# First attention: statistics begun a batch ahead, projections by part, and a top-k prologue laid into its last steps; second attention: values by chunk

## The chip, the cores and the metric

The kernel runs on one core of one Trainium2 chip. The core has five engines with a queue of instructions each: PE (TensorE, matrix products), DVE (VectorE), ACT (ScalarE), POOL (GpSimd) and SP (SyncE, which only issues transfers); they wait for one another through semaphores. The metric is the time of one launch on the device in microseconds; lower is better. All data is float32 unless a row says f16.

## The reference

A two-layer language-model tower over 4 sequences of 512 tokens with 128 features:

```python
h = tok(x, ids, numeric)                 # table rows gathered, added, + a small MLP
h = h + attn0(layernorm(h))              # 8 heads of 16; logits from qk and a distance (below)
h = h + topk_ffn(layernorm(h))           # 8 heads, 64 + 64 keys, top 8 of 64: 64 of 4096 rows per token
h = h + attn1(layernorm(h))              # 8 heads of 64, softmax in f32
h = h + moe(layernorm(h))                # 16 experts, each takes its top 64 tokens
# attn0:
omega = (q2[:, None] + k2[None, :] - 2*qk) / (exp(-nf_q) + 1)
A = softmax(qk / sqrt(16) - omega)       # nf_q: |Q - mean| summed, over Q's standard deviation
```

Here q2 and k2 are sums of squares over the 16 features of a head.

## The kernel before

A batch below is one sequence (B = 4), a tile is 128 tokens (TPB = 4 tiles a batch, 16 in all). The stages follow one another: a prologue (gathers, embedding, layer norm and projection of batch 0), the first attention, the top-k layer, the second attention, the experts. Each engine's program is one list written by hand; nothing reorders it. What an engine does beside the main loop is tied to a step number g or to u, the step within a batch, so an item that is not ready makes everything behind it on that engine wait.

**First attention.** It has 64 row steps, 16 a batch (STEPS0). In row step g PE makes the logits of 128 queries with 512 keys for two heads (L1529), DVE takes the two row maxima (L1038; PE's step g waits for the first maximum of step g-1). Twelve steps later (SHIFT) PE makes the same logits as columns with the maxima put in (L1533), and ACT takes their exps (L691, two a step). Values times weights (pv0, L1551) go into every second step. So row steps are 0 to 63, column steps 12 to 75, and steps to END0 = 84 finish the outputs. One PSUM bank, bank 7, is shared by all side work, one item a step, named in the table BANK7_0: `xnT` (transposed layer norm), `qkv` (projection), `k`, `q`, `q2` (transposes of the augmented operands), `back`, `fwd`, `out` (output), `tile` (a tile for the top-k layer). PE's next item waits until another engine has emptied the one before (first_bank7_free).

For each batch from 1 on the path is: gathered rows are added to h (POOL add_tokens, L492 and L494, for batches 2 and 3; DVE embed_tokens for 0 and 1); layer norm (DVE ln_stats L937, POOL's power L471, POOL normalise0 L478 or DVE ln_scale L949); PE transposes and projects it, one tile of q, k and v together at a time; ACT copies it out (copy_raw); POOL adds the biases with 12 instructions (L516) and computes mean, deviation, variance and the sums of squares (query_keys, L391 to L397), and a power for the standard deviation (sigma0, L484); DVE and ACT make the factors of nf_q; only then can PE transpose the augmented keys (L1485) and queries (L1491) of the batch.

**Top-k layer.** A tile needs its key scores (L1626, L1627), eight maxima and their indices (DVE), the inner products with 32 groups of down rows (L1689; ACT's relu frees their two banks), one-hot masks (one_v L1229, w_v L1235, one_u L1241) and the products that use them (`spread`, L1709). Tile t+1's front part goes beside tile t; the front parts of tiles 0 and 1 stand ahead of the loop.

**Second attention.** It has 64 steps: PE's logits (L1751), DVE's maximum (L1327), ACT's exps (L859), POOL's division (L621), PE's transposes (L1762), which ACT (L868) and DVE (L1341) evacuate. After every fourth step stand the 8 products of values of two heads (pv1, L1776), then ACT copies them (outT1, L875). Projections of the next batch and layer norms (L949) lie at fixed u.

## Time and profile before

| | |
|---|---|
| runs of the kernel | 1163.49 us median of 3 (1157.9 to 1167.11) |
| profiled execution | 1167.85 us, of which its span 1166.0 |
| mean granted TensorE clock | 0.92 |
| busy share of PE / DVE / ACT / POOL | 84% / 70% / 43% / 36% |
| first attention, row steps | 48.73 to 239.03 us |
| its rest and the first masks of the top-k layer | 239.03 to 308.70 us |
| second attention | 729.34 to 1014.80 us |

All starts are microseconds from the start of the span. Busy time says how long an engine had an instruction under way; PE's instructions overlap, so 84% does not say that it runs at its peak. "Granted clock" is the share of TensorE's full clock that the chip allowed it in that stretch: 1.00 is the higher of two levels (2.4 GHz), 0.50 the lower (1.2 GHz).

### The profile page before, as it was taken

Reading aid. Unit: us, or ns where it says so; the run is one execution under the profiler, and the core shown is the slowest. Engines: PE = TensorE matmul, PEld = TensorE weight load, DVE = VectorE, ACT = ScalarE, POOL = GpSimd, SP = SyncE. Lnnn points to the kernel's source line nnn. Section 1 sums busy time; section 2 is a strip of 40 time slices with the busy share of each in tenths; the row PEclk is TensorE's granted clock in tenths of the full one; section 3 lists DMA queues with packets and bytes.
Section 4 is the critical chain, followed back from the end, with each engine's and each line's share of the span. In section 5 each row is a group of like instructions: output and inputs, shape, how many; then the busy total and the mean of one; then the engine's idle time right before and its main releaser. Section 6 shows DMA issues by size and latency. Waiting matters only on the chain.

```text
span 1166.0 us, 21877 instructions
## 1 busy us (share of the span) xinstructions
PE 976.9 (84%) x8088; PEld 691.4 (59%) x8088; DVE 814.8 (70%) x2576; ACT 500.0 (43%) x1045; POOL 424.0 (36%) x398
## 2 busy tenths in 40 slices
PE   3486788897788889888888877899999988789997
PEld 3344344444577878777788875545455554367775
DVE  5655657655799999999999953565655565352887
ACT  1114445543434334444443332556555654335332
POOL 5468726200343343445333340445444453300000
PEclk9577889997799999999999998889999998879999
DMA  4000300000000000000000011000000000000000
GB/s 106 9 19 17 147 1 1 2 1 1 2 1 1 2 2 1 2 1 2 1 1 2 2 38 73 1 1 1 1 1 1 1 1 1 1 1 1 10 9 18
DMA packets 6720, 14.11 MB, mean 12 GB/s; under 512 B 1885, under 2 KB 4766, under 8 KB 6046
## 3 DMA queue, kind: packets, MB, share of 16 engines
q1 hardware_dynamic: 5598, 10.70, 2.8%
q0 software_dynamic: 1024, 2.10, 0.7%
q8 instruction: 62, 1.02, 0.4%
q14 instruction: 36, 0.29, 0.1%
HBM read 11.74 MB, written 1.05 MB: 11 GB/s over the span
## 4 chain that ended last, share of the span: by engine, by line
PE 49%; DVE 30%; issue 7%; ACT 6%; POOL 4%; POOLq 2%; DVEq 1%; DMA 0%; SPq 0%; ACTq 0%
PE bank L1776 5%; PE quad L1869 5%; PE bank L1864 5%; DVE w_v L1235 5%; PE quad L1751 4%; DVE i L1152 4%; PE bank L1762 3%; PE quad L1709 3%; PE bank L1529 3%; DVE one_u L1241 3%; PE bank L1720 3%; ACT a_e L859 2%; DVE a_negmax L1327 2%; PE bank L1689 2%; PE bank L1551 2%
## 5 line engine op out<-in xcount | busy, mean ns | idle before, releaser
L621 POOL TENSOR_TENSOR a_e<-a_e,a_rrec 128x1024 f32<-128x1024 f32 x64 | 121.2, 1893 | 165.8 <-DVE a_rrec L1334 165.7
L586 POOL TENSOR_TENSOR vals<-relu_in,g_sb 128x512 f32<-128x512 f32 x80 | 125.3, 1609 | 152.4 <-DVE one_u L1241 129.4
L1689 PE MATMUL bank<-xnT,wd 128*128 128x128 f32 x1024 | 136.8, 291 | 37.0 <-ACT relu_in L739 36.3
L1689 PEld LDWEIGHTS bank<-xnT,wd 128*128 128x128 f32 x1024 | 126.8, 201 | 45.0 <-ACT relu_in L739 43.9
L1720 PE MATMUL bank<-wu,vals 128*128 128x128 f32 x1024 | 118.7, 277 | 4.9 <-issue 4.9
L1720 PEld LDWEIGHTS bank<-wu,vals 128*128 128x128 f32 x1024 | 117.3, 194 | 4.9 <-issue 4.9
L859 ACT ACTIVATE a_e<-quad,a_negmax 128x512 f32<-128x512 f32 x128 | 86.9, 684 | 59.7 <-DVE a_negmax L1327 57.1
L1327 DVE TENSOR_REDUCE a_negmax<-quad 128x2 f32<-128x1024 f32 x64 | 77.7, 1215 | 42.3 <-PE quad L1751 41.4
L691 ACT ACTIVATE a_eT<-quad 128x512 f32<-128x512 f32 x128 | 69.6, 596 | 79.2 <-PE quad L1533 79.2
L1529 PE MATMUL bank<-a_kT,a_qT 32*128 32x512 f32 x344 | 88.4, 468 | 17.1 <-DVE a_q_aug L1038 10.9
L739 ACT ACTIVATE relu_in<-bank 128x512 f32<-128x512 f32 x128 | 73.2, 593 | 40.0 <-PE bank L1689 39.6
L1869 PEld LDWEIGHTS quad<-wu,hidT 128*128 128x128 f32 x512 | 67.6, 194 | 31.3 <-issue 27.8
L1533 PE MATMUL quad<-a_q2T,a_kT 32*128 32x512 f32 x512 | 83.8, 447 | 2.7 <-ACT a_eT L691 2.6
L1038 DVE TENSOR_REDUCE a_q_aug<-bank 128x1 f32<-128x512 f32 x86 | 57.1, 685 | 36.4 <-PE quad L1529 19.0
L1751 PE MATMUL quad<-a_kT,a_qT 64*128 64x512 f32 x512 | 79.1, 429 | 2.6 <-ACT a_e L859 1.9
L1762 PE MATMUL bank<-ident,a_e 128*128 128x128 f32 x512 | 72.8, 287 | 7.9 <-DVE a_eT L1341 4.3
L1709 PE MATMUL quad<-w_v,one_u 128*128 128x64 f16 x2048 | 70.9, 194 | 9.9 <-DVE one_u L1241 8.1
L1709 PEld LDWEIGHTS quad<-w_v,one_u 128*128 128x128 f16 x2048 | 65.9, 98 | 20.4 <-DVE one_u L1241 12.5
L1529 PEld LDWEIGHTS bank<-a_kT,a_qT 32*128 32x128 f32 x344 | 50.4, 213 | 44.1 <-DVE a_q_aug L1038 28.6
L1762 PEld LDWEIGHTS bank<-ident,a_e 128*128 128x128 f32 x512 | 57.5, 145 | 32.0 <-issue 22.6
L1241 DVE TENSOR_TENSOR one_u<-iota_u,uv 128x2048 f16<-128x2048 f16 x64 | 73.9, 1213 | 0.0
L1751 PEld LDWEIGHTS quad<-a_kT,a_qT 64*128 64x128 f32 x512 | 44.8, 191 | 47.9 <-issue 35.6
(238 smaller groups left out, 1944.1 us busy)
## 6 DMA issues: line engine op xcount, KB each, us to landing
wd<-in_pk_down SPq DMA_DIRECT2D x1, 2048.0 KB, 7.9
wu<-in_pk_up SPq DMA_DIRECT2D x1, 2048.0 KB, 12.5
wu<-in_moe_w SPq DMA_DIRECT2D x2, 1024.0 KB, 5.8
out<-h SPq DMA_DIRECT2D x4, 256.0 KB, 2.3
wd<-in_num_rows SPq DMA_DIRECT2D x1, 512.0 KB
a_eT<-in_pk_wqT SPq DMA_DIRECT2D x1, 512.0 KB, 7.1
a_eT<-in_pk_keys SPq DMA_DIRECT2D x1, 512.0 KB, 8.6
wu<-in_event_table,idx_e POOLq DMA_INDIRECT x16, 2.6
```

The lines of the kernel that those rows point to most:

```text
L586: nc.gpsimd.tensor_tensor(*weigh_args(t, c, k, g_sb[:, slot, :])).then_inc(vals_pool, 1)
L621: nc.gpsimd.tensor_tensor(e1[:, g % 4], e1[:, g % 4], rrec1[:, g % 4].unsqueeze(2).to_broadcast([P, 2, S]), ALU.mult).then_inc(a1.nr, 1)
L859: nc.scalar.activation(e1[:, g % 4, r, :], quad[:, 2 * (g % 2) + r, :], ACT.Exp, bias=negmax1[:, g % 4, r:r + 1], accum_out=rowsum1[:, g % ...
L1241: V.tensor_tensor(one_u[:, c * n:(c + 1) * n], iota_u[:].unsqueeze(1).to_broadcast([P, n, NU, 2]), token_pairs(uv[:, t % 2, 0, c * GT:(c + ...
L1327: V.tensor_reduce(negmax1[:, g % 4], quad[:, 2 * (g % 2):2 * (g % 2) + 2, :], AX.X, ALU.max, negate=True).then_inc(a1.mx, 1)
L1529: row = mm(bank[S1_BANKS[(2 * g + r) % 3]], qT0[part, qp, gr % 2, j * P:(j + 1) * P], kT0[part, kp, gr % 4, :], start=(n == 0), stop=(n == 3))
L1689: last = mm(bank[g % 2][:, q * P:(q + 1) * P], wd[:, IG * g + q, :], xnT_tile(t), start=True, stop=True)
L1709: made = mm(quad[:, 2 * (c % 2) + i // half_pair, cols], one_u[:, pair // 2, :, pair % 2], w_v[:, pair // 2, k, :, :, pair % 2].rearrange( ...
L1720: last = mm(bank[6][:, 0:D], vals[:, v, :], wu[:, v, :], start=(v == 0), stop=(v == NV - 1))
L1751: last = mm(quad[:, 2 * (g % 2) + r, :], qT1[rows, qp, p, j * P:(j + 1) * P], kT1[rows, kp, p, :], start=(n == 0), stop=(n == len(parts) - 1))
L1762: last = tp(bank[r][:, c * P:(c + 1) * P], e1[:, g % 4, r, c * P:(c + 1) * P], ident[:])
L1869: last = mm(bank[2 + e % 2][:, j * D:(j + 1) * D], hidT[:, e % 2, j * P:(j + 1) * P], w2e[:, e, :], start=True, stop=True)
```

## The change

- Projections of the first attention go by part: first q of all four tiles, then k, then v, with a semaphore for each; POOL adds one bias a part (three instructions of 128x512 a batch for twelve of 128x128). The shared-bank items of a batch move to earlier steps.
- POOL no longer adds gathered rows (add_tokens) nor normalises (normalise0): DVE does both, for batch 1 ahead of the loop, for batches 2 and 3 at steps 6, 12, 19 and 21. The two sums of squares go from POOL to DVE (square_sums, u = 7). POOL's gathers of batch 2 come right after the statistics of batch 1, its gathers of batch 3 after scale_queries(1).
- ACT's copy out of bank 7 stands between the two exps of a step.
- Into batch 3 and the steps after it go the transposes and scores of the top-k tiles 0, 1 and 2; into steps 66 to 73 the inner products of tile 0, one group of four a step. DVE's maxima and indices of tiles 0 and 1 spread over steps 64 to 79.
- Second attention: the values of a pair of heads are multiplied a chunk at a time, two products in each of four steps instead of eight in one; the copy of the sums moves one pair later and the output projection from u = 4 to u = 7.

```diff
-            {2: ("xnT", 1), 3: ("qkv", (1, 0)), 5: ("qkv", (1, 1)), 6: ("qkv", (1, 2)), 7: ("qkv", (1, 3)),
...
+            {0: ("xnT", 1), 1: ("qkv", (1, 0)), 2: ("qkv", (1, 1)), 3: ("qkv", (1, 2)), 9: ("q2", 0), 10: ("k", 2),
+             12: ("k", 3), 13: ("xnT", 2), 14: ("qkv", (2, 0)), 15: ("q", 2)},
...
+            {1: ("q2", 3), 2: ("back", 1), 4: ("fwd", 0), 5: ("q", 5), 6: ("out", 0), 8: ("k", 6), 9: ("q2", 4),
+             10: ("back", 2), 12: ("k", 7), 15: ("q", 6)},
+            {1: ("q2", 5), 2: ("back", 3), 3: ("tile", 0), 4: ("fwd", 1), 5: ("q", 7), 6: ("out", 1), 7: ("score", (0, 0)),
+             8: ("score", (0, 1)), 9: ("q2", 6), 10: ("back", 4), 11: ("tile", 1), 12: ("score", (1, 0)),
+             13: ("score", (1, 1))},
+            {1: ("q2", 7), 2: ("back", 5), 4: ("fwd", 2), 6: ("out", 2), 7: ("tile", 2), 8: ("score", (2, 0)),
+             9: ("score", (2, 1)), 10: ("back", 6), 12: ("uvp", 0), 15: ("back", 7)},
...
+        EARLY_INNER = range(ALL0 + 2, ALL0 + 2 + NG)
...
-        V1_AT = {3: 0, 7: 1, 10: 2, 11: 3}
+        V1_AT = {3: 0, 10: 1, 11: 2, 14: 3}
...
-            if u == 4 and 0 < b < B:
+            if u == 7 and 0 < b < B:
...
-            def add_tokens(b):
-                span = slice(b * S, (b + 1) * S)
-                pool.wait_ge(gath[b], 16 * 2 * TPB)
-                pool.wait_ge(h_early, b + 1)
-                nc.gpsimd.tensor_tensor(ev_rows[:, span], ev_rows[:, span], vv_rows[:, span], ALU.add)
-                pool.drain()
-                nc.gpsimd.tensor_tensor(h[:, span], h[:, span], ev_rows[:, span], ALU.add).then_inc(h_ready, 1)
...
-            def add_qkv_bias(b):
+            def add_qkv_bias(b, part, dst, done):
+                pool.wait_ge(a0.raw, 3 * (b - 1) + part + 1)
+                nc.gpsimd.tensor_tensor(dst, raw0[:, part], qkv_bias(part), ALU.add).then_inc(done, 1)
...
+            def query_keys(b):
                 pool.wait_ge(aug_clear, 1)
+                pool.wait_ge(a0.q_aug, b)
+                add_qkv_bias(b, 0, q4[:], a0.q_biased)
+                pool.drain()
+                sum_by_halves(pool, st0[:, 0], q4, dev)
                 pool.wait_ge(a0.k_ps, GROUPS * b)
...
-                sum_by_halves(pool, st0[:, 0], q4, dev)
+                add_qkv_bias(b, 1, k_aug[:, :, :, 0:DH0], a0.k_biased)
...
-                pool.wait_ge(a0.squares, 2 * b + 1)
-                sum_by_halves(pool, k_aug[:, :, :, K2], k2, k2).then_inc(a0.k_aug, 1)
                 sigma0(b)
-                pool.wait_ge(a0.squares, 2 * b + 2)
-                sum_by_halves(pool, st0[:, 8], q2, q2).then_inc(a0.q2, 1)
+                if b >= 3:
+                    pool.wait_ge(a0.pv, GROUPS * TPB * (b - 2))
+                add_qkv_bias(b, 2, v0[:, b % 3, :, :, 0:DH0], a0.v_biased)
+                if b >= 2:
+                    pool.wait_ge(a0.q2_ps, GROUPS * (b - 1))
+                nc.gpsimd.memset(q_aug[:, b % 2, :, :, TOPMOST], 0.0)
...
             rstd_step(lnB, 1, TPB)
-            normalise0(1)
-            add_bias0(0)
             gather(2)
             query_keys(1)
-            add_tokens(2)
+            rstd_step(lnB, 2, TPB)
             scale_queries(pool, nc.gpsimd, 1)
-            rstd_step(lnB, 2, TPB)
-            normalise0(2)
             gather(3)
-            add_tokens(3)
+            add_bias0(0)
             add_bias0(1)
             rstd_step(lnB, 3, TPB)
             query_keys(2)
             add_bias0(2)
+            add_bias0(3)
             scale_queries(pool, nc.gpsimd, 2)
             query_keys(3)
-            add_bias0(3)
...
-            def exp0(s):
...
+            def exp0(s, r):
                 pair, c = s // TPB, s % TPB
...
+                if r == 0:
+                    act.wait_ge(a0.cols, s + 1)
+                    if pair >= 3:
+                        act.wait_ge(a0.pv, (pair - 3) // 2 * TPB + c + 1)
+                nc.scalar.activation(eT0[:, pair % 3, r, c, :], bank[S2_BANKS[(2 * s + r) % 3]],
+                                     ACT.Exp).then_inc(a0.ex, 1)
...
-                    exp0(g - SHIFT)
+                    exp0(g - SHIFT, 0)
...
+                if SHIFT <= g < ALL0 + SHIFT:
+                    exp0(g - SHIFT, 1)
...
+                    if u == 5:
                         squares0(b + 1)
-                    if u == 13:
+                    if u == 12:
                         exp_nf(b + 1)
...
+                if g in EARLY_INNER:
+                    relu_inner(0, g - EARLY_INNER[0], g - EARLY_INNER[0] + 1)
+                if g == ALL0 + 5:
                     expand_indices(0)
+                if g == ALL0 + 6:
                     softmax_exp(0)
-            relu_inner(0, 0, NG)
-            copy_uvpT(0)
-            expand_indices(1)
-            softmax_exp(1)
-            copy_xnT_tile(2)
-            copy_scores(2)
+                if g == ALL0 + 11:
+                    expand_indices(1)
+                if g == ALL0 + 14:
+                    softmax_exp(1)
...
-                if g >= PV_LAG + 1 and (g - PV_LAG - 1) % TPB == 0:
-                    outT1((g - PV_LAG - 1) // TPB)
+            for g in range(STEPS_ALL + PV_LAG + 1):
+                if g >= PV_LAG + TPB and (g - PV_LAG) % TPB == 0:
+                    outT1((g - PV_LAG) // TPB - 1)
...
+            def add_first_bias(part, dst, done):
+                dve.wait_ge(a0.qkv, part + 1)
+                V.tensor_tensor(dst, quad[:, part, :].rearrange("p (j h d) -> p j h d", j=TPB, h=H), qkv_bias(part),
+                                ALU.add).then_inc(done, 1)
+            add_first_bias(0, q4[:], a0.q_biased)
+            add_first_bias(1, k_aug[:, :, :, 0:DH0], a0.k_biased)
...
+            square_sums(0)
             distance0(0)
...
+            add_first_bias(2, v0[:, 0, :, :, 0:DH0], a0.v_biased)
+            embed_tokens(1)
+            ln_stats(lnB, TPB, TPB)
...
+            ln_scale(lnB, 1, TPB, TPB)
             for g in range(GROUPS):
                 query_lo(g, bank[1 - g])
-            embed_tokens(1)
...
-                    if u == (11 if b == 0 else 9):
+                    if u == 7:
+                        square_sums(b + 1)
+                    if u == 8:
                         distance0(b + 1)
-                    if u == (13 if b == 0 else 12):
+                    if u == 12:
                         nf0(b + 1)
-                    if u == (14 if b == 0 else 13):
+                    if u == 13:
                         factors0(b + 1)
-                if g == STEPS0 - 2:
-                    dve.wait_ge(lnB.xn, 2)
-                    dve.wait_ge(h_ready, 3)
-                    ln_stats(lnB, 2 * TPB, TPB)
-                if g == STEPS0 + 6:
-                    dve.wait_ge(lnB.xn, 3)
-                    dve.wait_ge(h_ready, B)
-                    ln_stats(lnB, 3 * TPB, TPB)
-                if g == STEPS0 + 8:
-                    dve.wait_ge(lnB.ps, 3)
-                    ln_scale(lnB, 3, 3 * TPB, TPB)
-                if g == 3 * STEPS0 + 3:
+                if g in (6, STEPS0 + 3):
+                    n = 2 if g == 6 else 3
+                    embed_tokens(n)
+                    ln_stats(lnB, n * TPB, TPB)
+                if g in (12, STEPS0 + 5):
+                    n = 2 if g == 12 else 3
+                    dve.wait_ge(lnB.ps, n)
+                    ln_scale(lnB, n, n * TPB, TPB)
+                if g == 2 * STEPS0 + 8:
                     ln_stats(lnC, 0, TPB)
...
-            for g in range(ALL0 + 3):
+            for g in range(ALL0 + 1):
                 first_step(g)
             dve.wait_ge(consts, 2)
             half_max(0)
+            for g in range(ALL0 + 1, ALL0 + 3):
+                first_step(g)
             half_index(0, 0, 2 * H)
-            for g in range(ALL0 + 3, ALL0 + 7):
-                first_step(g)
             pair_scores()
             pair_max(0)
             pair_index(0)
-            for g in range(ALL0 + 7, ALL0 + 11):
+            for g in range(ALL0 + 3, ALL0 + 7):
                 first_step(g)
             positions(0)
             expert_numbers(0)
             half_max(1)
-            for g in range(ALL0 + 11, ALL0 + 16):
-                first_step(g)
             half_index(1, 0, 2 * H)
-            for g in range(ALL0 + 16, END0):
+            for g in range(ALL0 + 7, ALL0 + 11):
                 first_step(g)
             pair_scores()
             pair_max(1)
             pair_index(1)
+            for g in range(ALL0 + 11, ALL0 + 16):
+                first_step(g)
             positions(1)
             expert_numbers(1)
+            for g in range(ALL0 + 16, END0):
+                first_step(g)
             one_v_half(0, 0)
             one_v_half(0, 1)
...
-            def project_qkv(b, j, dst):
+            def project_qkv(b, part, dst):
                 pe.wait_ge(lnB.sb, b + 1)
-                mm(dst, xnT[:, j * P:(j + 1) * P], wqkv0[:], start=True, stop=True).then_inc(a0.qkv, 1)
+                for j in range(TPB):
+                    last = mm(dst[:, j * D:(j + 1) * D], xnT[:, j * P:(j + 1) * P], wqkv0[:, part * D:(part + 1) * D],
+                              start=True, stop=True)
+                last.then_inc(a0.qkv, 1)
...
-                        pe.wait_ge(v0_first, 1)
-                    else:
-                        pe.wait_ge(a0.qkv_biased, b + 1)
+                    pe.wait_ge(a0.v_biased, b + 1)
...
+                if g in EARLY_INNER:
+                    n = g - EARLY_INNER[0]
+                    if n == 0:
+                        pe.wait_ge(a0.mx, 2 * ALL0)
+                        pe.wait_ge(ld_exp, 32)
+                    if n >= 2:
+                        pe.wait_ge(relu_rdy, n - 1)
+                    inner_group(0, n)
...
-            inner(0, 1)
-            transpose_uvp(0)
-            scores(2, 1)
-            transpose_uvp(1)
...
-            def pv1(pair):
+            def pv1(pair, c):
...
-                        cols = slice((2 * p + r) * DH1, (2 * p + r + 1) * DH1)
...
+                if c == 0:
+                    pe.wait_ge(a1.ev_act, (pair + 1) * TPB)
+                    pe.wait_ge(a1.ev_dve, (pair + 1) * TPB)
+                    if p == 0:
+                        pe.wait_ge(v1_sb, (b + 1) * TPB)
+                    if pair:
+                        pe.wait_ge(a1.ots, pair)
+                for r in range(2):
+                    cols = slice((2 * p + r) * DH1, (2 * p + r + 1) * DH1)
+                    last = mm(bank[6][r * DH1:(r + 1) * DH1, :], v1[:, b % 2, c, cols], eT1[:, pair % 2, r, c, :],
+                              start=(c == 0), stop=(c == TPB - 1))
+                if c == TPB - 1:
+                    last.then_inc(a1.pv, 1)
...
-                if g >= PV_LAG and (g - PV_LAG) % TPB == 0:
-                    pv1((g - PV_LAG) // TPB)
+                if g >= PV_LAG:
+                    pv1((g - PV_LAG) // TPB, (g - PV_LAG) % TPB)
```

How it moves instructions is seen at three places. POOL, from the standard deviation of batch 0 to the statistics of batch 1 (a_st statistics, a_q and a_k_aug the query and augmented key, wu the gathered rows), before:

```order
L484 TENSOR_TENSOR a_st<-a_st,phalf 128x32
L471 TENSOR_TENSOR rstd<-veps,mhalf 128x4
L478 TENSOR_SCALAR xn<-h,mv,rstd 128x128 x4
L499 TENSOR_TENSOR h<-h,bo 128x512
L462 DMA wu<-in_event_table,idx_e 128x128
L462 DMA wu<-in_value_table,idx_v 128x128
...
L511 MEMSET a_q_aug 128x32
L516 TENSOR_TENSOR a_q<-a_raw,bqkv 128x128
L516 TENSOR_TENSOR a_k_aug<-a_raw,bqkv 128x8x16
L516 TENSOR_TENSOR a_v<-a_raw,bqkv 128x8x16
```

and after:

```order
L482 TENSOR_TENSOR a_st<-a_st,phalf 128x32
L478 TENSOR_TENSOR rstd<-veps,mhalf 128x4
L469 DMA wu<-in_event_table,idx_e 128x128
L469 DMA wu<-in_value_table,idx_v 128x128
...
L494 TENSOR_TENSOR a_q<-a_raw,bqkv 128x512
L398 TENSOR_TENSOR a_dev<-a_q 128x32x8
L402 TENSOR_TENSOR a_dev<-a_dev 128x32x4
L402 TENSOR_TENSOR a_dev<-a_dev 128x32x2
L404 TENSOR_TENSOR a_st<-a_dev 128x32
L494 TENSOR_TENSOR a_k_aug<-a_raw,bqkv 128x32x16
```

The normalisation and the residual bias are gone from ahead of the eight gathers, and the first statistics stand behind one bias instead of twelve. PE, the end of the first attention, before:

```order
L1570 MATMUL bank<-wo,a_oT 128x128 x4
L1689 MATMUL bank<-xnT,wd 128x128 x32
L1678 MATMUL bank<-ident,uvp 128x128 x4
L1616 MATMUL bank<-ident,xn 128x128
L1626 MATMUL bank<-keyw,xnT 128x512
```

and after, from step 65 on:

```order
L1535 MATMUL bank<-a_eT,a_v 32x512 x4
L1629 MATMUL bank<-xnT,wd 128x128 x4
L1520 MATMUL quad<-a_q2T,a_kT 128x512 x8
L1629 MATMUL bank<-xnT,wd 128x128 x4
L1520 MATMUL quad<-a_q2T,a_kT 128x512 x8
L1548 MATMUL bank<-ident,a_o 128x128 x4
L1535 MATMUL bank<-a_eT,a_v 32x512 x4
```

The 32 inner products that stood behind the last output projection lie four at a time between the column logits. PE in the second attention, around a batch's boundary, before:

```order
L1776 MATMUL bank<-a_eT,a_v 64x512 x8
L1751 MATMUL quad<-a_kT,a_qT 128x512 x8
L1762 MATMUL bank<-ident,a_e 128x128 x8
L1785 MATMUL bank<-wd,xnT 128x512
L1751 MATMUL quad<-a_kT,a_qT 128x512 x8
L1762 MATMUL bank<-ident,a_e 128x128 x8
L1782 MATMUL bank<-xnT,wd 128x512
```

and after:

```order
L1765 MATMUL bank<-a_eT,a_v 64x512 x2
L1740 MATMUL quad<-a_kT,a_qT 128x512 x8
L1751 MATMUL bank<-ident,a_e 128x128 x8
L1775 MATMUL bank<-wd,xnT 128x512
L1765 MATMUL bank<-a_eT,a_v 64x512 x2
L1740 MATMUL quad<-a_kT,a_qT 128x512 x8
L1751 MATMUL bank<-ident,a_e 128x128 x8
L1772 MATMUL bank<-xnT,wd 128x512
```

Each step now ends with two of the eight products.

## Rows read from the trace of the kernel before

**Rows 1.** Windows, by stage: us, busy us (instructions) of each engine, granted clock, DMA share, GB/s.

```profile
core 0: us, PE busy (x) PEld busy (x) DVE busy (x) ACT busy (x) POOL busy (x), PEclk, DMA share, GB/s
48.73:103.67 54.94, 39.29 (x220) 24.46 (x221) 31.52 (x68) 12.37 (x24) 38.66 (x53) 0.72 0.04 10
103.67:157.36 53.69, 41.75 (x356) 21.73 (x357) 31.49 (x62) 24.82 (x48) 37.29 (x52) 0.81 0.24 89
157.36:200.90 43.54, 38.09 (x374) 19.30 (x374) 28.52 (x52) 24.53 (x48) 22.39 (x36) 0.96 0.01 1
200.90:239.03 38.13, 32.91 (x352) 16.87 (x352) 24.80 (x49) 19.77 (x38) 7.38 (x11) 0.96 0.01 2
239.03:308.70 69.67, 52.55 (x301) 31.11 (x301) 36.40 (x198) 28.94 (x62) 2.84 (x6) 0.80 0.00 1
...
729.34:794.29 64.95, 58.85 (x312) 32.21 (x312) 36.94 (x63) 36.30 (x88) 30.58 (x17) 0.89 0.00 1
794.29:865.85 71.56, 67.75 (x383) 36.85 (x382) 40.84 (x71) 40.74 (x98) 32.47 (x18) 0.95 0.00 1
865.85:932.30 66.45, 64.61 (x381) 36.14 (x380) 36.35 (x58) 40.73 (x98) 31.51 (x17) 1.00 0.00 1
932.30:1014.80 82.50, 65.37 (x385) 39.69 (x384) 43.86 (x95) 39.80 (x96) 36.31 (x21) 0.87 0.00 1
```

**Rows 2.** Timeline, PE: start, us, line, operation, count [idle before <-releaser].

```profile
26.10 5.49 PE L1504 MATMUL quad<-wqkv,xnT 128*128 128x384 f32 x8 [0.67 <-ACT xnT L650]
...
89.86 1.09 PE L1485 MATMUL bank<-ident,a_k_aug 128*128 128x128 f32 x4 [5.06 <-POOL a_k_aug L397]
...
101.60 0.63 PE L1491 MATMUL bank<-ident,a_q_aug 128*128 128x128 f32 x4 [2.20 <-POOL a_q_aug L402]
```

**Rows 3.** Timeline, POOL, batches 0 and 1 (the first is one of 8).

```profile
59.21 1.10 POOL L462 DMA_INDIRECT wu<-in_event_table,idx_e  x1 [0.18 <-issue]
...
89.67 5.46 POOL L484 TENSOR_TENSOR a_st<-a_st,phalf 128x32 f32<-128x32 f32 x1
...
117.86 1.28 POOL L492 TENSOR_TENSOR wu<-wu 128x512 f32<-128x512 f32 x1 [1.59 <-DMA wu<-in_value_table,idx_v]
```

**Rows 4.** Windows, DVE alone: embedding and statistics of batch 1.

```profile
48.54:51.65 3.11, 2.79 (x13) 0.50 0.00 0
```

**Rows 5.** Timeline, DVE, first attention.

```profile
148.67 0.83 DVE L1007 TENSOR_SCALAR a_st<-a_st 128x32 f32<-128x32 f32 x1
...
150.01 0.18 DVE L1011 TENSOR_SCALAR a_st<-a_st 128x32 f32<-128x32 f32 x1
...
219.76 0.69 DVE L1038 TENSOR_REDUCE a_q_aug<-quad 128x1 f32<-128x512 f32 x1 [0.41 <-PE bank L1529]
```

**Rows 6.** Timeline, PE, from the last column steps to the top-k loop.

```profile
269.00 0.66 PE L1558 MATMUL bank<-ident,a_oT_raw 128*128 128x128 f32 x4
...
270.58 1.19 PE L1533 MATMUL quad<-a_q2T,a_kT 32*128 32x512 f32 x8
271.70 2.78 PE L1551 MATMUL bank<-a_eT,a_v 128*32 128x512 f32 x24
...
285.27 10.21 PE L1689 MATMUL bank<-xnT,wd 128*128 128x128 f32 x64 [0.78 <-DVE h L961]
...
308.71 1.51 PE L1709 MATMUL quad<-w_v,one_u 128*128 128x64 f16 x25 [4.99 <-DVE one_u L1241]
```

**Rows 7.** Windows, PE alone: the two score halves of a tile at full clock.

```profile
246.60:248.97 2.37, 2.37 (x10) 1.00 0.00 0
```

**Rows 8.** Timeline, DVE: the first mask product of the top-k layer.

```profile
303.09 4.42 DVE L1235 TENSOR_TENSOR w_v<-one_v,psp 128x8192 f16<-128x8192 f16 x1
```

**Rows 9.** Timeline, PE, second attention: the values of a pair in two batches.

```profile
788.55 3.65 PE L1776 MATMUL bank<-a_eT,a_v 128*64 128x512 f32 x16
...
842.89 5.82 PE L1776 MATMUL bank<-a_eT,a_v 128*64 128x512 f32 x16
```

**Rows 10.** Timeline, DVE, second attention.

```profile
849.90 1.22 DVE L1327 TENSOR_REDUCE a_negmax<-quad 128x2 f32<-128x1024 f32 x1 [3.33 <-PE quad L1751]
...
960.06 1.11 DVE L949 TENSOR_SCALAR xn<-h,mv,rstd 128x128 f32<-128x128 f32 x4 [3.05 <-POOL rstd L471]
```

196 lines of the change are left out of this document (69 added, 127 removed).

## The prediction

> **What bounds the kernel now.** I read the windows by stage first, because the change touches two attentions and the join between them and the top-k layer, and nothing in the top-k loop's or the experts' steady part. In [rows 1] the reader should compare two columns, the length of a stretch and PE's busy time in it, and then the granted clock. The third batch of the second attention lasts 66.45 with PE busy 64.61 at clock 1.00: PE is the bound there and nothing is idle. The second batch has the same work (383 matmul records for 381) and lasts 71.56. The first attention's batches 2 and 3 leave PE idle 5.45 of 43.54 and 5.22 of 38.13; batches 0 and 1 leave it idle 15.65 of 54.94 and 11.94 of 53.69, at clocks of 0.72 and 0.81. The join, 239.03 to 308.70, has no long wait on one engine: PE 52.55 busy of 69.67, DVE 36.40.
>
> Next the timeline of PE, for what ends its waits. In batch 0 the two long ones end with POOL: 5.06 for the sums of squares in the augmented keys, 2.20 for the scaled queries [rows 2]. POOL's timeline says why they are late [rows 3]: the biases and statistics of batch 1 stand behind eight gather issues (1.10 and a gap of 0.18 each, so 10.2). In the second attention the timeline shows the eight products of a pair as one block, 3.65 at full clock and 5.82 in a stretch at the lower one [rows 9], and DVE idle 3.33 behind that block for its next logits [rows 10].
>
> **The change, part by part.** The sum is made against the profiled execution, 1167.85 (span 1166.0 and 1.85 around it); the median of the runs is 4.36 less.
>
> *Prologue: -1 (-2 to +3).* The first bias waits only for q's third of the 5.49 projection instead of all of it [rows 2], about 3.7 earlier by thirds, but the second waits for k's two thirds; I count 2 for the chain. Against it DVE does embedding, statistics (3.11 [rows 4]) and normalisation (1.11, the same operation in [rows 10]) of batch 1 before the first logits instead of after them. GpSimd's power of 5.46 [rows 3] is under way there and DVE has to wait for it anyway, so most is covered; without that cover it would be 4.2 less the 2. Low end: the 2.
>
> *Batch 0: -6 (-9 to -1).* Gone: waits of 5.06 and 2.20, 7.3 together [rows 2], and the lower clock after them (four key transposes took 1.09 there [rows 2] and the same form 0.66 later [rows 6]; I give 1.5 to the steps behind). Also gone from the first steps are the 3.11 of batch 1's embedding, which I count at 1.5 since logits went on beside it. Added: batch 2's embedding and statistics at step 6, 3.11 less DVE's slack of about 0.4 a step (0.41 before a maximum [rows 5]) over two steps, +2.3; two sums of squares, by the nearest row of that size 0.69 each [rows 5], less slack, +1.0; normalisation at step 12, 1.1 less slack, +0.7. -10.3 + 4.0 = -6.3. High end: statistics later than needed by the length of a power.
>
> *Batch 1: -5 (-12 to +1).* With statistics in time it would look like batch 2, 43.54 for 53.69, which is -10. A new chain takes back half: gathers of batch 3 (10.2) now start after scale_queries(1), at about step 13, land some 1.6 after the last (by the wait in [rows 3]), so DVE's embedding at step 19 is in time only just and costs 3.11 less slack (+2.3), and POOL's statistics of batch 2 wait behind it: ACT's squares at u = 5 stand in the queue ahead of exps for some 2.5. The low end leaves the chain out and gives clock back; the high end has the embedding wait a further power.
>
> *Batch 2: -2 (-4 to +2).* Work of POOL goes (twelve biases for three), side items move earlier; PE idles only 5.45 [rows 1]. The statistics of the top-k layer's first batch come in.
>
> *Batch 3: +4 (+1 to +7).* Four score halves are added, 2.37 for two [rows 7], so 4.7, and two single transposes; a part falls into the 5.22 that PE is idle. High end: all of it and two DVE waits.
>
> *Join, to the first spread: -16 (-22 to -8).* Now PE's own sum decides. Twelve column steps at 1.19 [rows 6], 14.3; nine value products at 2.78/3 [rows 6], 8.3; eight inner groups at 10.21/8 [rows 6], 10.2 (this stretch ran at mixed clock); six transposes or projections at 0.66 [rows 6], 4.0; tile 2's two halves, 2.37 [rows 7]. That is 39.2 to the last column steps. Behind them stand the last output, transposes back and residual, which before took from the end of the 2.78 block at 274.5 to 285.27, 10.8 [rows 6]; positions and masks of tile 1 lie beside them, so I take 8. Then one_v (a quarter of w_v's elements, 1.1), w_v 4.42 [rows 8], and about 1.2 to the first spread (308.71 less 307.5). 39.2 + 8 + 6.7 = 53.9, for 69.67: -16. What is late next is DVE, which has 36.40 to do and no longer the 10 at 285.27 to wait through. High end: ACT's relu of a group delays the exp of its step by about 1 each, eight times.
>
> *Second attention: -17 (-25 to -4).* PE does the same products. What goes is the block: a quarter of it per step is 0.9, and DVE's maximum is not held for 3.33 [rows 10] once in four steps. Batch 1 falls to batch 2's 66.45 or a little under, -6 (-7 to -2). Batch 0: 64.95 with 312 records, against 64.61 x 312/381 = 52.9 if PE were all; I take half of the 12, -6 (-8 to -2). Batch 2 is at its floor: -1 (-2 to 0). Batch 3 (82.50, clock 0.87) keeps three layer norms on DVE that wait 3.05 for POOL [rows 10]; -4 (-8 to 0). The output projection at u = 7 and the later copy cost nothing while no item of bank 7 waits for them; the next pair's first product does wait for that copy, one step behind, 0.6 if uncovered, and that is in the ends.
>
> Sum: -1 - 6 - 5 - 2 + 4 - 16 - 17 = -43. 1167.85 - 43 = 1124.9, and against the median 1120.5.
>
> **A rule against the change.** The pair of tensor_scalar rows of one size in [rows 5], 0.83 and 0.18, differ in that GpSimd had an instruction under way until just before the first ended (a residual bias). I price it as a mechanism: each of the three embeddings and normalisations that move to DVE could be held to the end of a power of 5.46 [rows 3], 16.4 in all. The Trainium skill, SBUF — State Buffer, section Who interferes with whom, says that VectorE and GpSimd share a pair of ports as an exclusive lock, held for the whole instruction, which tensor_scalar may take and tensor_reduce does not; the 0.83 agrees with it. By that rule the sum would be 16.4 less of a gain; by the trace's tensor_scalar alone it is 0.65 an instruction, which the ranges above hold.
>
> **Rivals.**
> 1. DVE's added work is held beside GpSimd (the rule above): first attention's gain of 14 outside the join goes, 1120.5 + 16.4 = 1137. For it: [rows 5]. Against it: DVE idled in 23 of 55 us of batch 0 [rows 1]. Chance 0.13.
> 2. The block in the second attention only moved a wait: ACT and DVE evacuations pace the steps, only 2 is won, 1120.5 + 15 = 1135.5. For it: DVE's maximum and a wait of 3.05 on POOL remain [rows 10]. Against it: batch 2 is PE-bound in 64.61 of 66.45. Chance 0.12.
> 3. Both, 1152. Chance 0.05, of which about half is within 1% of no change.
> 4. More: the clock stays at full once the waits of batch 0 are gone. Batches 0 and 1 at 43.5 and 45 in place of 49 and 48.5, and the join at 49: -14 more, 1106; with batch 3 of the second attention at its low end 1102. Chance 0.08.
> 5. Slower: the lower clock spreads. PE's added pieces in batches 1 to 3 and the join make the steps uneven, PE waits a little in each, and the clock falls as in batch 0 (0.72). The block costs 5.82 for 3.65 there, 1.6 times [rows 9]. PE is busy 165.3 in these four stretches [rows 1]; at the lower level throughout it would bound them at 1.6 x 165.3 = 264 where I forecast 186, +78, so 1198. It takes over the gain of 43 when it holds in 55% of the stretch. Against it: clock 0.96 in batches 2 and 3 with PE as unevenly busy as now. Chance 0.05, of which 0.01 within 1%.
>
> That the change does not do what it says can be told from the order of instructions alone, which has the pieces where the words put them.
>
> **How the numbers follow.** Forecast 1120.5, chance 0.57. Its half-widths added as squares give about 13, so its own range is 1107 to 1134. Rivals 1 and 2 lie just above, rival 4 below; 1101 to 1141 takes them in and leaves out 3, 5 and the outer edge. About 1% is what a measurement of this kernel tells from no change (1152 to 1175). Faster: 0.57 + 0.13 + 0.12 + 0.08 and half of rival 3, 0.92. Same: 0.04. Slower: 0.04.
>
> **What would show it.** In the trace after: batch 0 near 49 without a wait of PE for POOL over 2; batch 1 near 48.5 with ACT's wait at u = 5 of batch 1; batch 3 near 42; 54 from step 64 to the first spread with no idle stretch behind the residual; in the second attention DVE's wait for logits behind the values under 1 and batch 1 at or under 66. I am wrong if the waits on POOL come back at another place, if the clock in batches 1 to 3 is under 0.8, if a relu of an inner group holds ACT's exps, or if the second attention's batches keep their lengths.

## The result, and the profile after

The changed kernel takes 1124.7 us (median of 4 runs, 1119.75 to 1131.43) where the kernel before takes 1163.95 (median of 4, 1157.9 to 1167.11). The ratio is 0.9663, 95% interval 0.9633 to 0.9692: faster by 39. Forecast were 1120.5 and the range 1101 to 1141. The profiled execution took 1123.27, of which its span 1121.3.

The windows of the changed kernel at the same events as [rows 1] (us, busy us and instructions of each engine, granted clock, DMA share, GB/s). The fifth, from the first logits of step 64 to the first spread, is called the join:

```profile
core 0: us, PE busy (x) PEld busy (x) DVE busy (x) ACT busy (x) POOL busy (x), PEclk, DMA share, GB/s
47.75:98.66 50.91, 41.24 (x249) 28.04 (x249) 32.14 (x65) 13.58 (x25) 24.25 (x26) 0.74 0.03 9
98.66:145.41 46.75, 37.28 (x384) 21.79 (x385) 31.84 (x66) 25.81 (x48) 30.26 (x34) 0.96 0.26 100
145.41:185.99 40.58, 33.27 (x365) 17.74 (x365) 30.39 (x63) 23.13 (x44) 15.84 (x17) 1.00 0.01 1
185.99:226.07 40.08, 36.91 (x366) 18.50 (x367) 23.58 (x40) 22.63 (x44) 4.78 (x9) 1.00 0.01 2
226.07:277.37 51.30, 40.45 (x287) 23.44 (x288) 36.15 (x198) 26.54 (x56) 2.67 (x6) 0.92 0.00 1
277.37:703.65 426.28, 367.45 (x4207) 328.67 (x4208) 382.91 (x1507) 166.27 (x350) 160.54 (x139) 0.94 0.03 9
703.65:763.65 60.00, 55.05 (x304) 30.40 (x305) 37.43 (x64) 36.38 (x89) 30.58 (x17) 0.94 0.00 1
763.65:830.41 66.76, 65.46 (x382) 34.98 (x381) 41.02 (x70) 40.50 (x99) 32.47 (x18) 1.00 0.00 1
830.41:895.30 64.89, 64.89 (x383) 34.92 (x382) 37.18 (x57) 40.69 (x99) 31.52 (x17) 1.00 0.00 1
895.30:973.08 77.78, 65.65 (x395) 36.59 (x393) 43.16 (x93) 39.24 (x96) 36.33 (x21) 0.93 0.00 1
```

Line by line against [rows 1]: batches 0 to 3 of the first attention 50.91, 46.75, 40.58 and 40.08 for 54.94, 53.69, 43.54 and 38.13; the join 51.30 for 69.67; the top-k loop 426.28 for 420.64; the second attention 60.00, 66.76, 64.89 and 77.78 for 64.95, 71.56, 66.45 and 82.50. The third batch of the second attention now has PE busy in all of its 64.89.

PE's timeline in the first attention, the answer to [rows 2] (start, us, line, operation, count, [idle before <-releaser]):

```profile
73.45 0.46 PE L1516 MATMUL bank<-a_kT,a_qT 32*128 32x512 f32 x1 [2.86 <-DVE a_q_aug L1026]
...
80.79 1.11 PE L1469 MATMUL bank<-ident,a_k_aug 128*128 128x128 f32 x4
...
120.63 0.47 PE L1516 MATMUL bank<-a_kT,a_qT 32*128 32x512 f32 x1 [3.65 <-ACT a_eT L671]
```

The transposes of batch 1's keys, which waited 5.06 for POOL [rows 2], wait for nothing at 80.79. Two new waits stand where the prediction looked for them: 2.86 ahead of PE's step 8, behind DVE's embedding of step 6, and 3.65 ahead of PE's step 23, behind ACT's work of step 21 (u = 5). ACT's and POOL's timelines tell the second one's story:

```profile
112.18 1.04 POOL L478 TENSOR_TENSOR rstd<-veps,mhalf 128x4 f32<-128x4 f32 x1 [5.17 <-DVE veps L924]
113.22 1.28 POOL L494 TENSOR_TENSOR a_q<-a_raw,bqkv 128x512 f32<-128x512 f32 x1
...
117.56 1.26 POOL L494 TENSOR_TENSOR a_k_aug<-a_raw,bqkv 128x512 f32<-128x512 f32 x1
```

```profile
118.85 0.63 ACT L639 ACTIVATE a_k<-a_k_aug 128x512 f32<-128x512 f32 x1 [3.17 <-POOL a_k_aug L494]
```

POOL waits 5.17 for the statistics of batch 3, the biases of batch 2 stand behind that, and ACT's squares, ahead of its exps, wait 3.17 for the second bias.

PE in the join, the answer to [rows 6] (an inner group in a step; the first spread):

```profile
245.79 1.16 PE L1629 MATMUL bank<-xnT,wd 128*128 128x128 f32 x8
...
277.37 2.85 PE L1702 MATMUL quad<-w_v,one_u 128*128 128x64 f16 x50 [6.19 <-DVE one_u L1223]
```

PE is 10.85 short of busy there, and 6.19 of that is one wait at the end, for the masks. DVE in the second attention, the answer to [rows 10] (the first row is the same step):

```profile
813.93 1.21 DVE L1311 TENSOR_REDUCE a_negmax<-quad 128x2 f32<-128x1024 f32 x1
...
921.30 1.11 DVE L931 TENSOR_SCALAR xn<-h,mv,rstd 128x128 f32<-128x128 f32 x4 [3.05 <-POOL rstd L478]
```

The maximum that waited 3.33 waits for nothing; in other steps up to 1.4 is left. The wait of 3.05 for POOL is there as before.

### The profile page after: what moved, and what is told of

Read it like the earlier page. It is cut to its first block, busy times and chain, and to the rows that moved or that the text cites. A ratio compares the mean times of both kernels' runs of the same rounds, so it can differ in the third digit from the quotient of the medians.

```text
span 1121.3 us, 21964 instructions
## 1 busy us (share of the span) xinstructions
PE 960.1 (86%) x8152; PEld 687.9 (61%) x8152; DVE 819.2 (73%) x2594; ACT 500.5 (45%) x1042; POOL 399.8 (36%) x335
## 4 chain that ended last, share of the span: by engine, by line
PE 53%; DVE 28%; issue 7%; ACT 6%; POOL 4%; DVEq 1%; POOLq 0%; DMA 0%; SPq 0%; ACTq 0%
PE quad L1859 5%; PE bank L1854 5%; PE quad L1740 4%; PE bank L1713 4%; DVE i L1134 4%; DVE w_v L1217 4%; PE bank L1765 4%; PE bank L1516 4%; PE bank L1751 4%; PE quad L1702 3%; PE bank L1629 3%; PE bank L1607 3%; PE bank L1535 2%; DVE one_u L1223 2%; ACT a_e L841 2%
## 5 line engine op out<-in xcount | busy, mean ns | idle before, releaser
L1629 PE MATMUL bank<-xnT,wd 128*128 128x128 f32 x1024 | 141.1, 295 | 33.9 <-ACT relu_in L717 33.8
L1629 PEld LDWEIGHTS bank<-xnT,wd 128*128 128x128 f32 x1024 | 130.2, 205 | 45.8 <-ACT relu_in L717 41.8
L841 ACT ACTIVATE a_e<-quad,a_negmax 128x512 f32<-128x512 f32 x128 | 86.8, 683 | 38.2 <-DVE a_negmax L1311 34.4
L1516 PE MATMUL bank<-a_kT,a_qT 32*128 32x512 f32 x344 | 83.7, 451 | 21.6 <-DVE a_q_aug L1026 13.4
L671 ACT ACTIVATE a_eT<-quad 128x512 f32<-128x512 f32 x128 | 73.9, 599 | 57.6 <-PE quad L1520 57.1
L717 ACT ACTIVATE relu_in<-bank 128x512 f32<-128x512 f32 x128 | 73.6, 593 | 40.9 <-PE bank L1629 40.4
L1859 PEld LDWEIGHTS quad<-wu,hidT 128*128 128x128 f32 x512 | 66.8, 192 | 31.0 <-issue 27.6
L1026 DVE TENSOR_REDUCE a_q_aug<-bank 128x1 f32<-128x512 f32 x86 | 57.1, 685 | 38.1 <-PE quad L1516 19.3
L1520 PE MATMUL quad<-a_q2T,a_kT 32*128 32x512 f32 x512 | 79.4, 428 | 0.8 <-ACT a_eT L671 0.7
L1516 PEld LDWEIGHTS bank<-a_kT,a_qT 32*128 32x128 f32 x344 | 47.4, 202 | 45.9 <-DVE a_q_aug L1026 27.8
```

The costliest lines, as they stand in the source:

```text
L841: nc.scalar.activation(e1[:, g % 4, r, :], quad[:, 2 * (g % 2) + r, :], ACT.Exp, bias=negmax1[:, g % 4, r:r + 1], accum_out=rowsum1[:, g % ...
L1516: row = mm(bank[S1_BANKS[(2 * g + r) % 3]], qT0[part, qp, gr % 2, j * P:(j + 1) * P], kT0[part, kp, gr % 4, :], start=(n == 0), stop=(n == 3))
L1520: col = mm(bank[S2_BANKS[(2 * s + r) % 3]], kT0[part, kp, gr2 % 4, c * P:(c + 1) * P], q2T0[part, qp, gr2 % 2, :], start=(n == 0), stop=(n ...
L1629: last = mm(bank[g % 2][:, q * P:(q + 1) * P], wd[:, IG * g + q, :], xnT_tile(t), start=True, stop=True)
L1859: last = mm(bank[2 + e % 2][:, j * D:(j + 1) * D], hidT[:, e % 2, j * P:(j + 1) * P], w2e[:, e, :], start=True, stop=True)
```

## The experiments

Each run was made beside the kernel before on the same chip. The stages of their profiled executions, from the first logits of steps 0, 16, 32, 48 and 64, the first spread, and the first logits of the second attention's steps 0 and 63 (its 63 steps in one column):

| run | batch 0 | 1 | 2 | 3 | join | top-k loop | second attention | ratio to before (95%) |
|---|---|---|---|---|---|---|---|---|
| before | 54.9 | 53.7 | 43.5 | 38.1 | 69.7 | 420.6 | 277.4 | 1 |
| changed | 50.9 | 46.8 | 40.6 | 40.1 | 51.3 | 426.3 | 260.4 | 0.9663 (0.9633 to 0.9692) |
| e1 values only | 58.6 | 51.9 | 42.0 | 38.2 | 67.2 | 423.2 | 260.2 | 0.9893 (0.9840 to 0.9947) |
| e2 first only | 49.5 | 48.4 | 40.6 | 40.1 | 51.4 | 419.6 | 268.7 | 0.9772 (0.9727 to 0.9818) |
| e3 block | 58.0 | 45.5 | 40.6 | 40.0 | 51.4 | 424.9 | 280.8 | 0.9823 (0.9776 to 0.9870) |
| e4 inner late | 49.5 | 46.8 | 40.6 | 40.1 | 48.0 | 423.0 | 260.3 | 0.9588 (0.9542 to 0.9634) |
| e5 spread | 47.8 | 47.3 | 40.6 | 40.1 | 51.1 | 423.2 | 262.4 | 0.9633 (0.9588 to 0.9677) |
| e6 statistics | 51.2 | 41.8 | 40.6 | 40.1 | 51.4 | 424.7 | 260.4 | 0.9601 (0.9557 to 0.9644) |
| e7 busy | 50.7 | 46.6 | 40.6 | 40.1 | 51.3 | 426.1 | 260.5 | 0.9656 (0.9613 to 0.9700) |
| e8 powers | 49.4 | 46.7 | 40.5 | 40.1 | 51.3 | 424.5 | 254.8 | 0.9633 (0.9590 to 0.9677) |
| e9 combined | 51.7 | 43.4 | 40.6 | 40.1 | 54.2 | 425.6 | 256.9 | 0.9561 (0.9518 to 0.9604) |
| e10 combined, busy | 48.5 | 43.5 | 40.6 | 40.1 | 54.4 | 425.8 | 256.7 | 0.9527 (0.9485 to 0.9570) |
| e11 tile 2 late | 49.1 | 46.6 | 40.5 | 40.1 | 52.2 | 425.3 | 260.4 | 0.9621 (0.9573 to 0.9668) |
| e12 sums on POOL | 49.4 | 47.9 | 40.5 | 40.1 | 51.4 | 425.1 | 260.4 | 0.9656 (0.9602 to 0.9711) |

The columns show how far one profile can be trusted: the top-k loop is 419.6 to 426.3, and 420.6 and 423.2 in the two runs whose first attention is as before; batch 0, the same in the changed kernel and in e2, e3, e4, e8 and e11, is 49.1 to 50.9 and once 58.0; batch 1, the same in these six, is 45.5 to 48.4; batches 2 and 3 repeat within 0.1 in the changed first attention. e2's profiled execution is the quickest of its six runs (1127.44 for a median of 1138.02), e3's the slowest of its four (1150.28 for 1144.74).

**e1, values only.** The kernel before with the second attention's hunks alone:

```diff
-        V1_AT = {3: 0, 7: 1, 10: 2, 11: 3}
+        V1_AT = {3: 0, 10: 1, 11: 2, 14: 3}
...
-            if u == 4 and 0 < b < B:
+            if u == 7 and 0 < b < B:
...
-                if g >= PV_LAG and (g - PV_LAG) % TPB == 0:
-                    pv1((g - PV_LAG) // TPB)
+                if g >= PV_LAG:
+                    pv1((g - PV_LAG) // TPB, (g - PV_LAG) % TPB)
...
```

> The kernel before with the second attention's part of the change alone (values of a pair two products a step, copy of the sums one pair later, output projection at u = 7, V1_AT). Theory (the block of eight products holds DVE's maximum and the clock): -17, from 1164 to about 1147, with the four batches of the second attention near 60, 66, 65 and 76, as in the changed kernel. Rival (the block only moved a wait; the gain in that stage of the changed kernel comes from what stands ahead of it): -2, about 1162.

Measured: 1151.34 for 1165.12, -13.8 (by the ratio's interval 6 to 19); its 63 steps took 260.2 for 277.4, -17.2. The theory holds in the stage. Batch 0, which is not touched, took 58.6 at a clock of 0.62 in this profile, and 54.9 at 0.72 in that of before.

**e2, first attention and join only.** The changed kernel with these hunks undone.

> The changed kernel with its second attention as before. Theory (the two parts are independent): 1164 - 26 = 1138, and the two gains of this run and of the one with the values alone add up to the whole, 39, within 4. In the stages: batches 0 to 3 near 51, 47, 41 and 40, the join 51. Rival (the first attention's gain comes back in the top-k loop, which was 5.65 longer in the changed kernel's trace): the top-k loop is again 5 or more longer than before's 420.6, and the whole gain here is 20 or less.

Measured: 1138.02, -27.1. With e1 that is 40.9 for the whole's 39.3, and the product of the two ratios, 0.9667, is close to the whole's 0.9663: within the intervals the parts add up. The top-k loop took 419.6. Its length goes with the granted clock there: 420.6 before and 419.6 here, both at 0.97, 426.3 in the changed kernel at 0.94, with DVE busy 382 to 384 in all three. So the 426.3 is not shown to be a price of the change.

**e3, the block again.** One edit in the changed kernel:

```diff
-                if g >= PV_LAG:
-                    pv1((g - PV_LAG) // TPB, (g - PV_LAG) % TPB)
+                if g >= PV_LAG and (g - PV_LAG) % TPB == 0:
+                    for c in range(TPB):
+                        pv1((g - PV_LAG) // TPB, c)
```

> The changed kernel with the eight products of a pair in one step again; the later copy, the output projection at u = 7 and the moved projections of V1_AT stay. Theory (cutting the block is what gains): most of the 17 goes back, about 1138 for 1125, with DVE waits of 3 for the logits behind the block. Rival (the moved side items gain, not the cutting): 1127 or less.

Measured: 1144.74, 20 slower than the changed kernel (19 by the ratios), more than was expected, and 280.8 in the second attention for 260.4. DVE's timeline has the wait back, once in most groups of four steps:

```profile
895.16 1.23 DVE L1311 TENSOR_REDUCE a_negmax<-quad 128x2 f32<-128x1024 f32 x1 [3.08 <-PE quad L1740]
```

What DVE's maxima wait for logits in all (us, times, the longest) says the same, before, changed and in e3:

```profile
DVE a_negmax L1327 <- PE quad L1751: 38.7, 21, 4.0
DVE a_negmax L1311 <- PE quad L1740: 21.4, 23, 4.0
DVE a_negmax L1311 <- PE quad L1740: 40.2, 21, 4.0
```

These waits are 17.3 less in the changed kernel, whose stage is 17.0 shorter, and 18.8 more in e3, whose stage is 20.4 longer. The moved side items alone give nothing: e3 with them takes 1144.74, e2 without them 1138.02. Whether the cut gains as much without them was not run. The block's second attention also varies, 268.7 (e2, these waits 30.7), 277.4 and 280.8 in three profiles, where the cut one repeats within 0.3 in most.

**e4, inner products late.**

```diff
-        EARLY_INNER = range(ALL0 + 2, ALL0 + 2 + NG)
+        EARLY_INNER = range(0)
...
                     softmax_exp(1)
+            relu_inner(0, 0, NG)
             copy_uvpT(1)
...
             pe.wait_ge(a0.add, B)
+            pe.wait_ge(ld_exp, 32)
+            for n in range(NG):
+                if n >= 2:
+                    pe.wait_ge(relu_rdy, n - 1)
+                inner_group(0, n)
             transpose_uvp(1)
```

> The changed kernel with the inner products of tile 0 behind the last output projection again, all in one row. Theory (PE's own sum decides the join; PE waits 6.2 for the one-hot masks at its end): the steps shorten by about 8, the 10 of the inner products lie beside DVE's masks and stand 10.8 where 7.8 of waits stood, so the join stays at 46 to 51 and the time at 1120 to 1125. Rival (moving the inner products into the steps is what gained): the join grows by 8 to 10, about 1134.

Measured: 1115.61, lower than the changed kernel and than the theory's 1120 to 1125, with the join at 48.0. In PE's timeline all 64 records stand in one row again, at full clock, and the wait for the masks is gone (the spread follows the transposes at once):

```profile
264.96 7.59 PE L1630 MATMUL bank<-xnT,wd 128*128 128x128 f32 x64 [1.36 <-DVE h L944]
272.39 0.39 PE L1625 MATMUL bank<-ident,uvp 128*128 128x128 f16 x4
272.61 2.10 PE L1708 MATMUL quad<-w_v,one_u 128*128 128x64 f16 x64
```

So laying the inner products into the steps is not what gained in the join. What did gain stands in the rows. Before, DVE waits 9.22 for ACT's exp of tile 1 (pe_), which stands in ACT's queue behind the eight relus of the inner products (the last of them is shown):

```profile
298.32 0.22 DVE L1182 TENSOR_REDUCE pz<-pe_ 128x8 f32<-128x64 f32 x1 [9.22 <-ACT pe_ L757]
```

```profile
295.52 0.60 ACT L739 ACTIVATE relu_in<-bank 128x512 f32<-128x512 f32 x1 [0.36 <-PE bank L1689]
...
298.04 0.24 ACT L757 ACTIVATE pe_<-pe_ 128x64 f32<-128x64 f32 x1
```

The masks follow that wait, and PE waits 4.99 for them [rows 6]. The changed kernel has the exp at step 78, ahead of the residual, and e4 leaves it there, though its relus are late again:

```profile
259.26 0.26 ACT L735 ACTIVATE pe_<-pe_ 128x64 f32<-128x64 f32 x1
```

```profile
261.02 0.21 DVE L1165 TENSOR_REDUCE pz<-pe_ 128x8 f32<-128x64 f32 x1
```

From the first inner product to the first spread e4 takes 7.7 for 23.4 before, 15.8 of the 21.7 that its join is shorter (2.6 of it because the inner products took 7.59 for 10.21, at a higher clock). PE's side of this is tile 2's scores, which stood behind the inner products too (e11). No run moved the exp alone.

e9 and e10 hold the same join as e4 and took 54.2 and 54.4: there the column steps, without the inner groups, ran at a lower clock (e9, PE's windows: start and end, length, PE's busy us and instructions, granted clock, DMA share, GB/s):

```profile
223.99:232.00 8.01, 7.47 (x55) 1.00 0.00 0
232.00:240.00 8.00, 6.52 (x34) 0.67 0.00 1
```

With the groups between the steps the join is 51.05 to 51.41 in all eight profiles, at clocks of 0.90 to 0.95; without them it is 48.0 (e4, at 0.96), 54.2 and 54.4 (both at 0.81). The clock is not what gained either: the join of before took 69.7 at 0.80 and 67.2 at 0.89 (e1).

**e5, the embedding in four steps.** DVE's two additions, statistics and their aggregation of batch 2 at steps 3, 4, 5 and 11 (embed_part does the k-th of the four):

```diff
+            EMBED_2, EMBED_3 = (3, 4, 5, 11), (19, 19, 19, 19)
...
-                if g in (6, STEPS0 + 3):
-                    n = 2 if g == 6 else 3
-                    embed_tokens(n)
-                    ln_stats(lnB, n * TPB, TPB)
+                for n, at in ((2, EMBED_2), (3, EMBED_3)):
+                    if g in at:
+                        embed_part(n, [k for k in range(4) if at[k] == g])
```

> The changed kernel with batch 2's embedding and statistics cut over steps 3, 4, 5 and 11 of the first attention in place of step 6. Theory (one long DVE item holds PE for 2.86 and the granted clock falls behind it, from 1.00 to 0.50 between 74 and 88): without it that stretch stays above 0.9, batch 0 takes 45 to 47 for 50.9, the time about 1120. Rival (DVE's total work in batch 0 counts, wherever it lies): batch 0 stays within 1 of 50.9 and the time at 1125.

Measured: 1119.31, near the 1120, with batch 0 at 47.8, above the 45 to 47. Step 7 takes 2.2 and not 5.1, so the stall of 2.9 was DVE's long item. But the clock fell all the same (PE's windows of e5):

```profile
72.00:76.00 4.00, 2.16 (x14) 0.85 0.00 0
76.00:80.00 4.00, 4.00 (x18) 0.50 0.02 4
```

The half of the theory that put the clock on that stall is wrong.

**e6, statistics of batch 3 early.**

```diff
             rstd_step(lnB, 2, TPB)
+            gather(3)
             scale_queries(pool, nc.gpsimd, 1)
-            gather(3)
...
+            EMBED_2, EMBED_3 = (6, 6, 6, 6), (14, 16, 16, 17)
```

> The changed kernel with batch 3's gathers ahead of scale_queries(1) on POOL, where it idles 14.7, and batch 3's embedding and statistics at steps 14, 16 and 17 in place of 19. Theory (the chain gathers, embedding, statistics, biases of batch 2 is what held batch 1 back: ACT waits 3.17 for the key bias, PE 3.7 for the exp behind it): both waits go, batch 1 takes 41 to 43 for 46.8, the time about 1121. Rival (POOL's queue is as long as before and the wait comes back at the next item, the statistics of batch 2): batch 1 within 1 of 46.8.

Measured: 1115.46, batch 1 at 41.8 for 46.8. ACT's squares (L639) no longer wait:

```profile
114.28 0.63 ACT L639 ACTIVATE a_k<-a_k_aug 128x512 f32<-128x512 f32 x1
```

PE's wait of 3.65 behind the exp is gone too, and no other has taken its place. The theory holds: the chain that the prediction priced at half of batch 1's gain was there, and was worth 5 in this profile (43.4 and 43.5 in e9 and e10, which hold the edit too).

**e7 and e10, added products.** e7 puts two, five and one product into PE's waits of the prologue, e10 seven for the five, and four in batch 0's steps, on top of e9:

```diff
+            def keep_busy(n):
+                for _ in range(n):
+                    mm(bank[5], ident[:], xnT[:], start=True, stop=True)
...
+            keep_busy(2)
             for g in range(GROUPS):
                 transpose_keys(g, bank[7 - g])
+            keep_busy(5)
             for g in range(GROUPS):
                 first_queries(g, bank[1 - g])
+            keep_busy(1)
```

> The changed kernel with eight added products of 128x512 that nothing reads, on PE where it waits in the prologue (two behind the projection, five behind the key transposes, one behind the query transposes). Theory (the first steps run at half clock because PE idled before them): the granted clock is 1.00 at the first step and steps 0 to 3 take 11 for 14.4, the time about 1121; if the clock does not rise in the prologue, the five products take 10 where 7.5 is idle and the start is 2 to 3 later. Rival (the lower clock of the first steps is not set by what PE did before): steps 0 to 3 stay at 14.4.

> The kernel of the four edits with more added products that nothing reads: seven in place of five behind the key transposes, so that PE does not idle before the query transposes, and one of 384 columns in each of steps 4, 6, 8 and 11 of batch 0, whose 0.8 us of waiting they fill. Theory (the clock falls where PE idles: with five products it was 0.97 to 44 us and 0.50 from 44 to 57.4, behind an idle stretch of 2.2): granted clock of 1.00 through steps 0 to 12, batch 0 at 40 to 43 for 48, time 5 lower than the kernel of the four edits. Rival (the clock of batch 0 does not follow what PE did before): 0.50 again from 44 to 57 and from 76 to 88, batch 0 at 48 or longer.

PE's windows of e7, and then of e10:

```profile
34.00:44.00 10.00, 5.39 (x18) 0.97 0.05 14
44.00:47.80 3.80, 3.34 (x10) 0.50 0.18 52
```

```profile
34.00:44.00 10.00, 8.80 (x22) 0.83 0.05 14
44.00:47.80 3.80, 2.45 (x14) 1.00 0.19 52
47.80:57.40 9.60, 9.40 (x60) 0.82 0.12 29
...
76.00:80.00 4.00, 4.00 (x22) 0.50 0.00 0
```

The query transposes in e7's timeline, and in e10's:

```profile
44.46 1.97 PE L1475 MATMUL bank<-ident,a_q_aug 128*128 128x128 f32 x8 [4.09 <-DVE a_q_aug L409]
```

```profile
44.60 1.09 PE L1497 MATMUL bank<-ident,a_q_aug 128*128 128x128 f32 x8 [0.68 <-DVE a_q_aug L409]
```

In e7 the clock was high while products ran and low behind the 4.09 that was still left idle (the 2.2 in e10's expectation was a misreading), so nothing changed: steps 0 to 3 took 14.4 as before. That its 1121.89 is near the theory's 1121 is chance. Behind 0.68 the same transposes took 1.09 for 1.97. In e10 the clock is 1.00 from 44.00 up to the first step; steps 0 and 1 take 1.98 and 4.68 for 3.05 and 5.71. From 76 to 80 it is 0.50 again, in spite of the fillers, and batch 0 at 48.5 missed the 40 to 43. e10 measured 1110.38, the lowest ratio of all; its gain over e9 lies within both intervals.

**e8, powers one step earlier.**

```diff
-                    if b == B - 1 and u + 1 in LN_E_AT:
-                        rstd_step(lnE, LN_E_AT[u + 1], TPB)
+                    if b == B - 1 and u + 2 in LN_E_AT:
+                        rstd_step(lnE, LN_E_AT[u + 2], TPB)
```

> The changed kernel with POOL's three powers for the last layer norm one step earlier in batch 3 of the second attention. Theory (DVE's three waits of 3.05 on POOL are on the path there): batch 3 takes 4 to 8 less, the time about 1119. Rival (PE's work of 63.6 sets that batch, the waits lie beside it): within 1 of 1125.

Measured: 1118.86; batch 3's steps took 65.4 for 68.7, -3.3, less than the theory's 4 to 8 and more than its rival's 1. (The other 2.3 of this run's shorter second attention lie in its batch 0, which the edit does not touch.) The three waits (3.05 each in the changed kernel) are gone, but the normalisation itself grew, because it now runs beside POOL's division. DVE's row and POOL's:

```profile
913.23 2.61 DVE L931 TENSOR_SCALAR xn<-h,mv,rstd 128x128 f32<-128x128 f32 x4 [0.26 <-POOL rstd L478]
```

```profile
913.10 1.89 POOL L600 TENSOR_TENSOR a_e<-a_e,a_rrec 128x1024 f32<-128x1024 f32 x1
```

2.61 for 1.11 is what a later start had avoided.

**e9, four edits together** (e4, e5, e6, e8).

> The changed kernel with four edits of the runs so far together: inner products of tile 0 late, batch 2's embedding over steps 3, 4, 5 and 11, batch 3's gathers and statistics early, the last layer norm's powers one step earlier. Theory (their stages lie one after another, so the gains add): stages of 48 (batch 0), 42 (batch 1), 48 (join) and 65.4 (batch 3 of the second attention) in one run, 3 + 5 + 3 + 3 = 14 below the changed kernel, 1108 to 1112. Rival (DVE bounds join and top-k loop together, so what PE gains there comes back): the top-k loop grows by 3 or more over 423 to 426, about 1114.

Measured: 1116.5, above the theory's 1108 to 1112 and, by the intervals, no better than e4 or e6 alone. Batch 3 of the second attention (65.2) and batch 1 (43.4) kept most of their gains; the join came at the lower clock; and in batch 0 (51.7, e5 alone 47.8) two edits got into each other's way. POOL's queue and DVE's:

```profile
82.95 1.03 POOL L478 TENSOR_TENSOR rstd<-veps,mhalf 128x4 f32<-128x4 f32 x1 [4.69 <-DVE veps L995]
84.15 1.09 POOL L469 DMA_INDIRECT wu<-in_event_table,idx_e  x1 [0.17 <-issue]
...
95.02 2.48 POOL L488 TENSOR_TENSOR h<-h,bo 128x512 f32<-128x512 f32 x2
```

```profile
95.57 2.49 DVE L982 TENSOR_TENSOR wu<-wu 128x512 f32<-128x512 f32 x1 [3.10 <-DMA wu<-in_value_table,idx_v]
```

POOL's power of batch 2 waits 4.69 for e5's statistics at step 11, and e6's gathers stand behind that power: they start at 84.15, DVE's embedding at step 14 waits 3.10 for their landing, and step 15 took 7.7 for 3.2. Neither theory nor rival had this.

**e11, tile 2 late**, with e4:

> The changed kernel with tile 0's inner products late and tile 2's transpose and scores behind them, as before the change. Theory (PE's chain behind the residual sets the join there, since DVE's masks end with the inner products): the steps shorten by 2.7, the chain behind grows by 2.4 and two waits of 1.0 to 1.3, so the join takes 49 to 51 for 48.0. Rival (what gained in the join is DVE's maxima and indices of tiles 0 and 1, laid between the steps; PE's order there matters little): within 0.7 of 48.0.

Measured: 1121.44 for e4's 1115.61, and a join of 52.2, above the theory's 49 to 51. The two ran on different chips, and the intervals of their ratios overlap, so the times alone do not decide. PE's rows do for the chain behind the residual:

```profile
264.11 8.95 PE L1632 MATMUL bank<-xnT,wd 128*128 128x128 f32 x64 [0.78 <-DVE h L946]
...
276.49 2.10 PE L1711 MATMUL quad<-w_v,one_u 128*128 128x64 f16 x64
```

It takes 12.4 for e4's 7.7; 1.4 of that are the inner products (8.95 for 7.59, at a lower clock), the other 3.4 tile 2's transpose and scores. The spread stands right behind them and no longer waits for the masks. That is the theory; the whole join varies by 6 with the clock.

**e12, sums of squares on POOL.**

```diff
+                pool.wait_ge(a0.squares, 2 * b + 1)
+                sum_by_halves(pool, k_aug[:, :, :, K2], k2, k2).then_inc(a0.k_aug, 1)
                 sigma0(b)
+                pool.wait_ge(a0.squares, 2 * b + 2)
+                sum_by_halves(pool, st0[:, 8], q2, q2).then_inc(a0.q2, 1)
...
-                    if u == 7:
-                        square_sums(b + 1)
```

> The changed kernel with the sums of squares of batches 1 to 3 on POOL again, ahead of and behind its power for the standard deviation, as before. Theory (of DVE's added work each 1.36 costs about 1.0 in its step, and the statistics begin early enough for POOL): batches 0 to 2 take 0.5 to 1 less each, 1123. Rival (the sums belong to what made the statistics late): PE waits for the augmented keys or queries again, batches 0 to 2 take 1 to 3 more each, 1128 or more.

Measured: 1123.41, batches 49.4, 47.9 and 40.5. In batch 2, which repeats within 0.1, the move of the sums neither cost nor gained. Batches 0 and 1 lie within what the same code showed in other profiles (49.1 to 50.9 and 45.5 to 48.4), so 1 in either would not be seen.

## Why the prediction was right, point by point

The prediction was right in sign and size: 39 for 43, and by the spans of the profiled executions 44.7 for 43. Some of the closeness is luck: the stages with a forecast gave 47.4 by the windows of [rows 1], the top-k loop took 5.6 back and the experts gave 3.0, and for neither of these was anything forecast. The half-widths of the terms, added as squares, are about 13 on the side of a greater gain, as stated, but 18 on the other; the range holds both.

- **Prologue**, forecast -1: 47.75 for 48.73.
- **Batch 0**, -6: -4.0, inside its ends. Both waits on POOL went. The stall of the embedding was priced at 2.3 and is 2.9 (e5). Two terms failed: for the sums of squares, 1.0, e12 shows no cost, and the 1.5 for a recovering clock did not come: the granted clock is 0.74 where it was 0.72.
- **Batch 1**, -5: -6.9. The chain was read right, to the ACT wait at u = 5 (forecast 2.5, measured 3.17); e6 shows that it costs 5.
- **Batch 2**, -2: -3.0. **Batch 3**, +4: +1.9; more of the added scores fell into PE's idle time than was allowed.
- **Join**, -16: -18.4, and the sum of PE's pieces, 53.9, is close to 51.30. The step on DVE, that it would no longer have the 10 at 285.27 to wait through, had the right wait, DVE's 9.22 (though the prediction found no long wait on one engine there), but not what ends it. The wait goes because ACT's exp of tile 1 stands ahead of the relus, not because the inner products lie elsewhere: with them back in one row it did not return, and the join took 48.0 (e4). In the changed kernel the masks stand alone at the end, the 6.19; in e4 the inner products run beside them. The other piece behind the residual is tile 2's scores, 3.4 in e11. How the remainder ahead of the residual divides among the moved scores and DVE's maxima and indices was not tried.
- **Second attention**, -17: to step 63 -17.2 in e1's stage and -17.0 in the changed kernel's, -16.0 by the windows of [rows 1]; e3 and DVE's waits for logits show that the cutting does it. By batches -5.0, -4.8, -1.6 and -5.7 to step 63, for -6, -6, -1 and -4.
- **Signs** that did not come: batch 1 of the second attention at or under 66 (66.8), DVE's waits for logits under 1 (up to 1.4), and no idle stretch behind the residual (the 6.19).

Of the rivals, 1 (DVE held beside GpSimd) did not come: the moved embedding ran at its own length beside the power. 2 is refuted by e1 and e3. With these two 3, which was both, falls. 4 and 5, on the clock, both stayed out: batches 1 to 3 ran at 0.96, 1.00 and 1.00, batch 0 as low as before. The price of rival 5, 5.82 for 3.65, was read as that of the lower level, but the clock was 0.62 over that block (before, 842.89 to 848.70), between the levels; at 0.50 eight transposes took 1.97 for 1.10 (e7, at 0.50 and at 0.97), which is 1.8 times. The top-k loop was 5.6 longer in the profiled run and 1.0 shorter in e2's, and went with the clock.

## What to carry to other kernels

A block of matrix products that is longer than the slack of the engine which waits for the next one is worth cutting into the steps even where PE is already busy: 17 us here in the profiled stage for the same products, and 13 to 20 between the medians of the runs. When work is moved off an overloaded queue, follow what the new queue puts behind it, the next gathers, statistics and biases in order; that chain took back 5 of batch 1's gain, and of two good edits that share such a queue one took back what the other had gained. And before crediting a moved piece with a gain, put it back alone: the inner products, the most visible part of the join, were not what gained. A small exp that stood behind their relus in ACT's queue held DVE for 9.22.

## What the runs showed of the hardware

In these rows the hold between DVE and POOL depends on what POOL runs, not on its being busy. In the prologue of the changed kernel DVE's addition of two SBUF tiles kept its length beside a power of 5.46:

```profile
34.30 5.46 POOL L482 TENSOR_TENSOR a_st<-a_st,phalf 128x32 f32<-128x32 f32 x1 [1.07 <-DVE a_st L1064]
```

```profile
36.50 0.68 DVE L969 TENSOR_TENSOR wu<-wu 128x512 f32<-128x512 f32 x1
```

The same addition took 2.49 beside POOL's two additions of 128x512 in e9, and a normalisation 2.61 for 1.11 beside its division in e8; each ended within 0.9 of POOL's. Which property of the power lets the addition through no run shows. The Trainium skill, SBUF — State Buffer, section Who interferes with whom, has VectorE with two SBUF inputs contend with a GpSimd instruction that reads SBUF: e9 agrees with it, the 0.68 beside the power does not.

The widest spreads between profiles went with the granted clock: the top-k loop took 419.6 at 0.97 and 426.3 at 0.94, and the same batch 0 took 49.1 to 50.9 at 0.71 to 0.74, and 58.0 at 0.59 in e3:

```profile
47.84:105.84 58.00, 49.69 (x248) 34.30 (x249) 33.14 (x65) 13.49 (x25) 23.72 (x26) 0.59 0.03 7
```

A gain of a few microseconds in a stage that runs at a mixed clock cannot be read from one profile of it.
